# Attention kernel: the transposed row maxima go into the query stack by one transfer issued by ScalarE, not by two on SyncE's queue through DRAM

## What is computed

```python
q = jnp.einsum('btd,hdk->bhtk', x, Wq)        # k, v alike
scores = jnp.einsum('bhqk,bhsk->bhqs', q, k) * scale
scores = jnp.where(causal, scores, -jnp.inf)
weights = jax.nn.softmax(scores, axis=-1)
out = jnp.einsum('bhqs,bhsk->bhqk', weights, v)
out = out.transpose(0, 2, 1, 3).reshape(x.shape[0], Tn, N_EMBD) @ Wo.T + bo
```

## Time and profile before

| | us |
|---|---|
| median of 3 runs | 1035.91 |
| lowest and highest | 1033.72, 1044.79 |
| the profiled execution | 1039.77 |
| its span, first to last instruction | 1038.0 |

### The profile page before, as it was taken

The page is one execution under the profiler, slowest core; times in us unless marked ns, Lnnn a source line. Parts: engine busy times, 40 slices in busy tenths (PEclk is TensorE's granted clock), DMA queues, the critical chain, the costliest instruction groups (busy, mean ns, idle before and its releaser), DMA issues. The chain is left out here.

```text
span 1038.0 us, 19725 instructions
## 1 busy us (share of the span) xinstructions
PE 710.9 (68%) x6652; PEld 481.9 (46%) x6652; DVE 582.1 (56%) x1765; ACT 344.1 (33%) x597; POOL 332.4 (32%) x654
## 2 busy tenths in 40 slices
PE   1799887889875229997225398467918886189991
PEld 0355455455554119996111144233404443178991
DVE  7878645889335807665504276336506762446673
ACT  2222233432433214442320156134405453134440
POOL 0122300134312746776430001101310313346771
PEclk9899998999985559999555599778958998589996
DMA  9101496011200115554321101100210000045554
GB/s 225 45 21 58 114 190 136 23 60 43 57 1 11 49 58 154 154 155 116 111 112 70 56 4 45 80 14 11 88 60 3 24 3 22 21 119 153 155 165 133
DMA packets 99568, 80.89 MB, mean 78 GB/s; under 512 B 7383, under 2 KB 91418, under 8 KB 98730
## 3 DMA queue, kind: packets, MB, share of 16 engines
q1 hardware_dynamic: 94926, 70.25, 25.2%
q0 software_dynamic: 4544, 9.38, 2.7%
HBM read 54.44 MB, written 23.40 MB: 75 GB/s over the span
## 5 line engine op out<-in xcount | busy, mean ns | idle before, releaser
L1210 DVE TENSOR_REDUCE rmax<-PA 128x1 f32<-128x512 f32 (+3 forms) x256 | 120.6, 489 | 165.5 <-PE PA L1895 158.8
L738 POOL DMA_INDIRECT rows_dram<-va,idx x64 | 64.0, 999 | 161.2 <-DVE va L1093 143.4
L753 POOL DMA_INDIRECT outs_dram<-va,ids x78 | 96.4, 1236 | 52.9 <-POOL ids L749 26.4
L1852 PE MATMUL PC<-ffn_w,pm 128*128 128x128 f32 x624 | 87.7, 283 | 8.8 <-DMA ffn_w<-in_w 8.3
L1893 PE MATMUL PA<-mqb,idb 128*128 128x128 bf16 x256 | 61.5, 241 | 44.8 <-DMA qst<-qst 29.5
L1895 PE MATMUL PA<-kst,qst 96*128 96x512 bf16 (+3 forms) x256 | 85.9, 342 | 0.0
L1563 ACT ACTIVATE pm<-PB 128x1024 f32<-128x1024 f32 (+1 forms) x64 | 45.0, 703 | 118.6 <-PE PB L1918 118.5
L1852 PEld LDWEIGHTS PC<-ffn_w,pm 128*128 128x128 f32 x624 | 75.7, 191 | 12.9 <-DMA ffn_w<-in_w 12.0
L1140 DVE SCALAR_TENSOR_TENSOR pm<-PB,invb,decay 128x512 f32<-128x512 f32 x78 | 58.2, 746 | 38.1 <-ACT decay L1476 37.9
L1893 PEld LDWEIGHTS PA<-mqb,idb 128*128 128x128 bf16 x256 | 26.1, 102 | 108.6 <-issue 59.7
L1468 ACT ACTIVATE kv_b<-P 128x256 f16<-128x256 f16 x78 | 29.9, 384 | 130.6 <-PE P L1831 130.6
(11 more groups left out here) (244 smaller groups left out, 1555.9 us busy)
## 6 DMA issues: line engine op xcount, KB each, us to landing
ffn_w<-in_w SPq DMA_DIRECT2D x78, 256.0 KB, 2.9
rows_dram<-wall SPq DMA_DIRECT2D x1, 8385.0 KB, 46.8
X<-in_w SPq DMA_DIRECT2D x32, 256.0 KB, 2.9
proj_w<-rows_dram SPq DMA_DIRECT2D x78, 65.0 KB
qst<-parts_dram SPq DMA_DIRECT2D x12, 384.0 KB
kst<-parts_dram SPq DMA_DIRECT2D x12, 384.0 KB
X<-in_x SPq DMA_DIRECT2D x8, 256.0 KB, 4.4
R<-outs_dram SPq DMA_DIRECT2D x4, 512.0 KB, 3.9
```

What stands on the lines that cost most here:

```text
L738: nc.gpsimd.indirect_dma_start(out=rows_dram, out_offset=bass.IndirectOffsetOnAxis(ap=idx[:, t, r:r + 1], axis=0), in_=xrow[:, t, :], in_o ...
L753: nc.gpsimd.indirect_dma_start(out=outs_dram, out_offset=bass.IndirectOffsetOnAxis(ap=ids[:, k % YB:k % YB + 1], axis=0), in_=ysb[:, k % Y ...
L1210: nc.vector.tensor_reduce(rmax[:, i, h % HG:h % HG + 1], PA[:, n % 2, 0:(i + 1) * P], AX_X, ALU.max).then_inc(pair_sb[n % 2], 1)
L1852: ins = mm(PC[:, k % 2, 0:D], eT[:, k % 2, f, :], w2b[k % WB2][:, f, :], start=f == 0, stop=f == FB - 1)
```

## The change

`maxima(g)` and the DRAM tensor `max_dram` are gone, with the semaphore `max_out`. Right behind its copy into `mxT`, ScalarE waits for that copy to be written and issues one transfer from `mxT` (12 partitions of 1 KB) to the three rows of `qst` (L1533 of the changed kernel). Its next copy into `mxT` waits for that transfer to have landed. SyncE's program in the attention is now `stacks(0)` to `stacks(3)` in a row, each still behind its own waits.

```diff
-            def maxima(g):
-
-                b = (g // NG) % 2
-                o = (g % NG) * HG * L
-                wait_pair(sp, "mx", g)
-                if g >= 1:
-                    sp.wait_ge(max_in, 16 * g)
-                sp.dma_start(max_dram, mxT).then_inc(max_out, 16)
-                sp.wait_ge(max_out, 16 * (g + 1))
-                sp.dma_start(qst[KQ:KQ + NP3, b, o:o + HG * L], max_dram.rearrange("(i h) n -> i (h n)", h=HG)
-                             ).then_inc(max_in, 16)
...
             stacks(0)
-            stacks(1)
-            for g in range(NG * SEQ):
-                maxima(g)
-                if g % NG == 0 and 1 <= g // NG < SEQ - 1:
-                    stacks(g // NG + 1)
+            for s in range(1, SEQ):
+                stacks(s)
...
                         if what == "mx":
                             if s >= 1:
-                                act.wait_ge(max_out, 16 * s)
+                                act.wait_ge(max_in, 16 * s)
                             ins = nc.scalar.activation(mxT, src[0:NP3 * HG, :], ACT.Copy)
...
                         ins.then_inc(pair_sb[n % 2], 1)
+                        if what == "mx":
+                            wait_pair(act, "mx", s)
+                            o = s % NG * HG * L
+                            act.dma_start(qst[KQ:KQ + NP3, s // NG % 2, o:o + HG * L], mxT).then_inc(max_in, 16)
```

More of the change, by code:

```diff
@@ L364, in mixer_kernel @@
         amax_dram = nc.dram_tensor("amax_dram", (P, E), F32, kind="Internal").ap()
-        max_dram = nc.dram_tensor("max_dram", (NP3 * HG, L), BF16, kind="Internal").ap()
         PA = ps("PA", [P, 2, 512])
@@ L412, in mixer_kernel @@
         st_in = (sem("st_ina"), sem("st_inb"))
-        max_out = sem("max_out")
         max_in = sem("max_in")
```

## The result

The changed kernel takes 1000.38 us (median of four runs, 998.03 to 1004.16) against 1040.35 of the kernel before beside it: ratio 0.9618, 95% interval 0.9577 to 0.966. That is 40 us less. The forecast was 41.9 us less, 996 us, in a range of 986 to 1015; it started from the 1039.77 and 1035.91 of the first three runs before. The profiled execution took 1001.85 us with a span of 1000.0, against 1039.77 and 1038.0: 38 us in the trace.

A forecast was written before the change was run, and what follows sets the result against it. TensorE waits for maxima queued behind stack transfers on SyncE. -13.9 - 16.4 - 16.0 + 2.4 + 2 = -41.9 us gives 997.9 from 1039.77 or 994.0 from 1035.91; forecast 996, range 986 to 1015.

The forecast's parts named there:

- Part 1: Maxima's path: two hops become one; 1.7 us at most per hop, worth 0 in the 13 groups without a wait.
- hidden anyway: Rival: the maxima land only when the stacks have, one hop of 1.68 us goes in three places; 1033, chance 0.07.
- Part 2: Maxima's transfer leaves SyncE's queue; its landing beside stack transfers bounded by 1.68 and 28.9 us, taken as about 5.
- The model of the turns: DMA engines beside stack loads: the maxima's small pieces alternate with single stack rows, not with whole stack transfers.
- Group 0: -13.9: Ahead of group 0: maxima landed by about 574, TensorE there at 577.81, the wait of 13.85 us goes whole.
- Group 5 to 6: -16.4: Group 5's 22.05 us wait goes, some 6.8 us for the stack comes; group 6 starts at 680.3 instead of 696.71.
- Group 9 to 10: -16.0: The same with sequence 3: the 22.71 us wait goes; group 10 starts at 773.4 instead of 789.37.
- Part 3: TensorE's cold clock behind the remaining waits before groups 6 and 10: 1.2 us each, +2.4; bounds 0 and 3 each.
- Part 4: ScalarE waits for its copy and issues 16 transfers: 0.45 us each, bounds 0.3 and 0.8; mostly covered, +2 in all.
- Partly late: Rival: small pieces alternate with whole stack transfers of 4.7 us, five being 23.5 us; 1015, chance 0.08.
- Held at the issue: Rival: ScalarE's issue is held until the stack has moved, groups 5 and 9 +10.5 us each; 1059, chance 0.05.
- ScalarE's issue is dear: Rival inside the forecast's range: issue at its upper bound and uncovered, +12.8 instead of +2; 1007, chance 0.10.

The follow-up runs named there:

- e1: Kernel before, with the maxima going from their copy straight into the query stack in one hop, still issued by SyncE at its old place: ratio 0.9992.
- e2: Changed kernel with the second hop put back: ScalarE writes the maxima to DRAM and reads them back on its own queue: 1006.06 us, ratio 0.9659.
- e3: e1 with the maxima of groups 5 and 9 issued ahead of the stack transfers in SyncE's queue: 1021.26 us, ratio 0.9801.
- e4: Changed kernel with the parts laid out in DRAM so that a stack transfer's 24 rows are one dimension: 989.08 us, ratio 0.9294.
- e11: e4 once more, beside the changed kernel on one chip: 985.18 us, ratio 0.9335.
- e9: e3 with the wide stack layout of e4, SyncE issuing everything: 982.21 us, ratio 0.9309.
- e10: The changed kernel once more, unchanged, in another batch: 1018.23 us, ratio 0.965 to the kernel before.
- e5: Kernel before with the wide stack layout of e4, ScalarE issuing nothing: 1000.77 us, ratio 0.9391.

## Why the prediction was right, point by point

**What bounds.** Right, and shown from both sides: e1 takes the hop away and leaves the waits (0.9992), e2 keeps both hops and loses the waits (0.9659), e3 loses two of three by order alone (0.9801). e3 keeps the third, group 0's. The reading that decided it was the 28.9 us between two issues of SyncE beside a DMA share of 0.19: a queue that is long on few engines.

**Part 1, the hops: 0.** Right (e1). The 5 us which I gave the hop in the rival *hidden anyway* were too much: in e1 the waits are 13.02, 19.41 and 22.70, together 3.5 us shorter, where I had 5, and the total shows nothing.

**Part 2, the landing beside the stacks: 3 to 5 us.** Too small for the transfer that the change makes. The trace's records of single packets show it: in the changed kernel the last packet of the maxima ended 7.80 us behind the issue for group 0, and 6.81 to 7.28 us for groups 1, 5, 6 and 10, whose transfers also ran beside stacks. The other eleven took 1.58 to 1.61. The model of the turns was right. The fifteen packets come in three streams of five, as the stack's do in three, and alternate one for one with packets of 16 KB and 0.61 us; from the first to the last they took 2.6 to 3.5 us. What the sum left out comes before: the first packet stands 3.9 to 4.4 us behind the issue beside stacks, and 1.4 alone. Each of e2's two hops took less, 4.9 and at most 5.1 us, but the two together are 10.

It was enough, with luck for group 0. The last packet ended at 577.03 and TensorE needed the maxima at 577.92, 0.9 us later; in e4 and e11, where TensorE did wait, its mask followed the last packet by 0.97 and 0.95 us. So nothing was to spare there, and a landing much later would have cost time. Group 5 had 6.9 us to spare, and group 9's transfer was issued at 710.59, before the stack transfers began at 711.02.

The page "DMA: Bandwidth & Descriptors" of the Trainium skill (Queues, rings and completion order) has each engine go round its queue rows packet by packet. The packet records agree, as said above.

The same page of the Trainium skill (Rules for kernel authors) says that spreading transfers over SP, ACT and GpSimd for bandwidth does not help, since they share the engines, and that it only saves issue time. That rule is on bandwidth; read as "behind the same backlog", as the prediction did, it would have given 1033, and that did not come. e3 and e9 agree with it in part: for groups 5 and 9 the second queue brings nothing that another order in one queue does not.

**Group 0: -13.9.** 13.74. **Group 5 to 6: -16.4.** 15.8. **Group 9 to 10: -16.0, and +1.2 for the cold start of group 6, which falls in between.** 14.0. The waits for the stack, 6.8 and 7.4 us by the forecast, were 6.01 and 8.03, but the mixture was another. Group 4 was 1.89 longer than I let it be, since the clock dipped, and this cost nothing, since the stack's wait behind it shrank: 6.01 where it would have been 7.9. What counts is only when the stack lands and what group 6 takes after.

**Part 3, the clock: 1.2 for each remaining wait.** Too small, and hidden in the length of the groups. Behind a wait of 6 us the changed kernel's clock was 0.50 for four microseconds and 0.55 after:

```profile
666.70:670.50 3.80, 3.80 (x18) 2.87 (x19) 1.38 (x2) 1.02 (x1) 0.00 (x0) 0.50 0.00 0
670.50:674.00 3.50, 3.50 (x22) 1.56 (x21) 1.38 (x2) 1.69 (x3) 0.00 (x0) 0.55 0.00 0
```

The first three slots of group 6 took 8.07 us, and those of group 10 8.01. In the kernel before and in e1, where these groups follow no wait, they took 5.90. So a cold start behind a short wait cost 2.2 and 2.1 us: the bound of 0 is excluded, and the cost lies between my 1.2 and the upper bound of 3. By the whole group it looks like 1.0 and 1.1 (19.6 us against 18.64 in group 6), because the kernel before lost time later in the same group, at a clock of 0.82 over the whole of it; in e1, at 1.00 throughout, group 6 took 714.92 - 698.79 = 16.13.

**Part 4, ScalarE: +2.** The sum came out near by luck, for it is made of other things. One issue with its wait costs ScalarE 0.9 us (1.39 against 0.48), above my upper bound of 0.8. Of the seven even groups one shows it, group 14, where no maxima products remain and ScalarE is in the chain. This is the changed kernel there:

```profile
813.31 0.57 ACT L1512 ACTIVATE decay<-PA 12x512 bf16<-12x512 f32 x1
813.91 0.73 ACTq L1533 DMA_DIRECT2D qst<-decay  x1
814.74 0.60 ACT L1541 ACTIVATE decay<-P 128x512 f32<-128x512 f32 x1 [0.86 <-ACT decay L1512]
```

Group 14 took 10.69 us instead of 8.72. Of these 1.97 us, 1.22 were lost in its first two slots, before this copy began, at a granted clock of 0.58 over the first 3.3 us; that is not the issue's doing. The slot of the issue took 3.08 us instead of 2.33. The issue's own part is plainer in e10, the same kernel at a granted clock of 1.00 over these slots. Its masks at both ends of the slot are

```profile
822.97 0.28 PE L1902 MATMUL PB<-mkb,idb 128*128 128x128 bf16 x2
826.28 0.27 PE L1902 MATMUL PC<-mkb,idb 128*128 128x128 bf16 x2
```

3.31 us apart, 0.98 more than in the kernel before (2.33); e4 has 3.31 too. The two slots ahead of it took 1.98 us in e10, e4 and the kernel before alike. So an early issue costs about 1 us in group 14. All six kernels with an early issue took 10.7 to 11.8 us there, the seven without it 8.71 or 8.72 in six and 9.59 in e3, where the clock was 0.60 at the start. What goes beyond the 1 us goes with dips of the granted clock in or behind the slot (0.53 from 827 to 829 in e10); whether the issue brings these about is open.

**Behind the attention: 0.** It was +2.5: from the start of group 15 to the end 177.16 us became 179.64. The second mixture of experts has no changed instruction. The same stretch took 185.04 us in e10, which is the same kernel, and 176.5 to 190.2 over all the kernels, so 2.5 us are within what it scatters by; why it scatters is not shown.

**The total.** Up to the start of group 10 the trace gained 43.5 us, where the forecast had 45.1. Behind it the forecast took back 3.2, for one cold start and ScalarE, and the trace 5.5: 1.1 in group 10, 2.0 in group 14 and 2.5 behind the attention. The mechanism was right, and so, within 2 us each, were the waits that go and come. The landing, the cold start and the issue were each taken too small, and that the sum was near in spite of it is partly luck: the landing just fitted into what group 0 had, and the cold starts were partly paid by dips that the kernel before had in the same groups.

**The rivals.** *Partly late* and *hidden anyway*: the longest landing was 7.80 us, a turn is one packet of 16 KB and not a whole stack transfer, and no wait for maxima is left. *Held at the issue*: the longest of 16 ScalarE issues was 1.33 us, the first one. *ScalarE's issue is dear*: it is, at 0.9 us, and covered everywhere but in group 14 as far as the group lengths tell.

## What to carry to other kernels

A small transfer that someone waits for must not stand behind a bulk load in the same queue; look at what was issued ahead of it, not at its size or its hops. A queue of its own cured that here, and where the transfer was ready before the bulk load was issued (groups 5 and 9), issuing it first did too, without costing a compute engine its time. Group 0's was ready only after the load was issued; there the own queue helped, or, in e5 and e9, the shorter load. The own queue does not make the transfer as fast as alone: it took 6.8 to 7.8 us beside the stacks instead of 1.6, and 11.0 to 12.6 beside those of the wide layout in e4 and e11. And when the wait is gone, look at why the bulk load was slow: here the DMA share was 0.19 during a long load, and a layout whose outermost dimension is 24 instead of 3 raised it to 0.69 and gave 33 us more, nearly as much as the change.

## What the runs showed of the hardware that was not expected

- A one-hop transfer from 12 partitions to 3 takes 0.73 us to issue on ScalarE (16 of them, 0.728 to 1.332) and 0.71 on SyncE in e1, where the write to DRAM and the read back took 0.29 and 0.23. The direct form was the dearer one to issue. The 1.332 is the first of the 16.
- Nearly four times the share of the engines brought 1.7 times the rate: 0.19 and 81 GB/s became 0.69 and 139 GB/s, with the same 16 KB rows. By these numbers each engine slowed to less than half (1.29 us for a packet of 16 KB instead of 0.61). Why was not tried.
- The same transfer of 12 KB took 1.58 to 1.61 us from issue to its last packet alone, 6.81 to 7.80 beside stack transfers of another queue, and 11.0 to 12.6 beside those of the wide layout. About half of the delay in the changed kernel, some 3 us, lies before its first packet.
- The granted clock dips without an idle stretch: 0.79 over eight fully busy microseconds of group 4 in two of the kernels above, and 1.00 in the kernel before, with the same instructions for TensorE. Such dips went with group lengths that differ by 2 us in group 4 (17.6 to 20.0) and 5 us in group 6 (16.1 in e1, 21.3 in e10, a wait's cold start included), and make the lengths of single groups a poor measure of an edit.
